# Attention units of a post-norm decoder: score rows as (sequence, query), values on both halves of the partitions, one output product, masks per token

## What is computed

```python
def _L2_xattn_ref(q, k, v, Wqkv, bqkv, Wo, bo, key_padding_mask, attn_mask, n_heads):
    proj = (jnp.concatenate([q, k, v], axis=1) @ Wqkv + bqkv)   # per head: qp, kp, vp
...
    scores = jnp.einsum('bqhd,bkhd->bhqk', qp, kp) / np.sqrt(dh).astype(qp.dtype)
    scores = jnp.where(mask, NEG, scores)
    attn = jax.nn.softmax(scores, axis=-1)
    y = jnp.einsum('bhqk,bkhd->bqhd', attn, vp)
    return y.reshape(Bq, T1, Dm) @ Wo + bo

x = _layernorm(x + _L0_attn_ref(x, ...))           # first mixing, "a0"
x = _layernorm(x + _L0_xattn_ref(ctx, x, ctx, ...))   # x0
x = _layernorm(x + _L0_ffn_ref(x, ...))            # two local-attention layers
x = _layernorm(x + _L1_attn_ref(x, W_qkv))         # a1
x = _layernorm(x + _L1_xattn_ref(x, ctx, ctx, ...))   # x1
x = _layernorm(x + _L1_ffn_ref(x, ...))            # "g", "gelu"
x = _layernorm(x + _L2_attn_ref(x, ...))           # "ema"
x = _layernorm(x + _L2_xattn_ref(x, ctx, ctx, ..., 32))  # x2
x = _layernorm(x + _L2_ffn_ref(x, ...))            # experts, top 1
x = _layernorm(x + _L3_attn_ref(x, ..., rel_emb))  # a3: scores + relative positions, causal
x = _layernorm(x + _L3_xattn_ref(x, ctx, ctx, mask, ...))  # x3
x = _layernorm(x + _L3_ffn_ref(x, ...))            # experts, top 2
```

## Time and profile before

| | |
|---|---|
| median of 3 runs | 818.88 us (815.96 to 819.70) |
| span of the profiled execution | 819.0 us |
| PE busy | 678.8 us, 83% |
| PEld busy | 523.5 us, 64% |
| DVE busy | 587.6 us, 72% |
| ACT busy | 462.2 us, 56% |
| POOL busy | 440.3 us, 54% |

### The profile page before, as it was taken

One profiled execution on the slowest core, in us unless ns is written; L12 is line 12 of the kernel. 1 busy time (PEld: TensorE's weight loads), 2 busy tenths in 40 slices (PEclk: granted clock), 3 DMA queues, 4 the chain that ended last, 5 costly groups with the idle time before them and its releaser, 6 DMA issues.

```text
span 819.0 us, 21672 instructions
## 1 busy us (share of the span) xinstructions
PE 678.8 (83%) x8144; PEld 523.5 (64%) x8144; DVE 587.6 (72%) x1594; ACT 462.2 (56%) x1136; POOL 440.3 (54%) x591
## 2 busy tenths in 40 slices
PE   5887968899988997999986799885978988955990
PEld 2576735777867785777743677645955666644990
DVE  4876969899888855788748987752557878862554
ACT  2235647487887662776722775443826756731671
POOL 3268726676655732254415877424666657553450
PEclk8667988799999998899995999867989989965995
DMA  8069000000000000000007700004124563004112
GB/s 340 11 222 136 2 1 2 1 1 2 2 1 2 1 2 1 2 3 3 4 1 87 224 3 2 3 13 98 46 59 155 182 184 103 3 30 98 58 38 84
DMA packets 49317, 45.21 MB, mean 55 GB/s; under 512 B 12896, under 2 KB 39648, under 8 KB 48704
## 3 DMA queue, kind: packets, MB, share of 16 engines
q1 hardware_dynamic: 46976, 39.23, 17.8%
q0 software_dynamic: 2240, 4.60, 1.6%
HBM read 30.94 MB, written 12.88 MB: 54 GB/s over the span
## 4 chain that ended last, share of the span: by engine, by line
PE 52%; DVE 18%; issue 10%; POOL 8%; ACT 5%; DMA 4%; SPq 1%; DVEq 0%; ACTq 0%; POOLq 0%
PE bank L889 6%; PE bank L868 6%; PE bank L877 5%; PE bank L904 3%; PE bank L1152 3%; PE bank L1078 3%; PE bank L1159 2%; PE bank L986 2%; DVE pairs L1721 2%; DVE pairs L1717 2%; POOL slots_x L2078 2%; PE bank L963 2%; DMA rel_scratch<-G 1%; PE bank L795 1%; PE bank L1012 1%
## 5 line engine op out<-in xcount | busy, mean ns | idle before, releaser
L2063 POOL TENSOR_TENSOR sm<-sm,mx 128x512 f32<-128x512 f32 x80 | 84.0, 1053 | 44.2 <-DVE mx L1638 43.7
L1251 ACT COPY pT<-bank 128x512 f32<-128x512 f32 x112 | 65.5, 585 | 46.3 <-PE bank L877 45.5
L1246 ACT ACTIVATE pr<-sm 128x512 f32<-128x512 f32 x112 | 70.2, 634 | 20.2 <-POOL sm L2063 19.6
L877 PE MATMUL bank<-W,pr 128*128 128x128 f32 x448 | 73.9, 290 | 8.3 <-ACT pT L1251 6.6
L2030 POOL TENSOR_SCALAR veps<-mv 128x1 f32<-128x1 f32 x104 | 25.3, 243 | 97.2 <-DVE mv L1573 97.1
L868 PE MATMUL bank<-pairs,Q 64*128 64x256 f32 x448 | 68.6, 427 | 2.2 <-DVE sm L1635 0.8
L2058 POOL TENSOR_TENSOR pairs<-KS,quad 128x512 f32<-128x512 f32 x48 | 50.5, 1054 | 35.5 <-ACT KS L1228 35.5
L2031 POOL TENSOR_TENSOR rstd<-veps,W 128x1 f32<-128x1 f32 x104 | 60.7, 584 | 8.7
L877 PEld LDWEIGHTS bank<-W,pr 128*128 128x128 f32 x448 | 52.0, 146 | 20.6 <-issue 10.8
L889 PEld LDWEIGHTS bank<-VX,pT 64*64 64x64 f32 x3072 | 52.1, 140 | 13.0 <-issue 6.8
L889 PE MATMUL bank<-VX,pT 64*64 64x9 f32 (+1 forms) x3072 | 56.5, 204 | 3.6 <-ACT pT L1251 1.6
(11 more groups left out here) (403 smaller groups left out, 1901.6 us busy)
## 6 DMA issues: line engine op xcount, KB each, us to landing
big<-gup SPq DMA_DIRECT2D x4, 1024.0 KB, 10.0
rel_scratch<-G SPq DMA_DIRECT2D x16, 256.0 KB, 2.7
W<-small SPq DMA_DIRECT2D x1, 3206.5 KB, 12.2
big<-early SPq DMA_DIRECT2D x2, 1557.0 KB, 8.4
slots_x<-zero SPq DMA_DIRECT2D x2, 1472.0 KB, 26.3
big<-down SPq DMA_DIRECT2D x8, 256.0 KB, 8.8
QM<-rel_scratch SPq DMA_DIRECT2D x16, 128.0 KB, 2.7
PM<-rel_scratch SPq DMA_DIRECT2D x16, 128.0 KB, 2.8
```

Source lines behind the costliest of these rows:

```text
L877: last = pe.transpose(tile(ps, p), pr[:, u % 2, 4 * h + p, :, :].rearrange("p b k -> p (b k)"), ident)
L1246: act.activation(pr[:, u % 2, 4 * h:4 * h + 4, :, :].rearrange("p g b k -> p b g k"), sm[:, 2 * (u % 2) + h, :].rearrange("p (b g k) -> p ...
L1251: act.copy(pT[:, u % 2, 4 * h:4 * h + 4, :], bank[BK[f"tu{h}"]][:, :].rearrange("p (h n) -> p h n", h=4)).then_inc(pt_ready, 1)
L2063: tt(v, v, bc(mx[:, slot, :], [P, 8, S], 2), ALU.subtract).then_inc(pcentered, 1)
```

## The change

The score rows become (sequence, query): one unit now computes its scores with eight products of 64x64 in place of four of 64x128, sequence b on its half of the partitions, and the two parities c of the heads as column halves. The exponent's output then needs no swap. The values of the two parities e stand on the two halves of the partitions (four products of 64 tokens in place of one; their bias is laid out the same way in a new table `BV`, filled by twelve small copies on DVE, and left out where it is zero). The 32 products of va give rows (sequence, query), in banks 6 and 7, and one reciprocal and one product of DVE normalise both banks. The output product is one product of 128x128 with the weights as they are, their rows only permuted at loading (sixteen loads, all at the start, with no memset before them). Masks are kept for each token row: half the columns, the two sequences loaded to the two halves of the partitions. The PSUM banks become one tensor; several steps change banks. The early routing of x3 becomes five planned steps (lg, e1, e2, rk, sl), and all ranks of the planner are new.

```diff
@@ plan @@
-            "pe.va": 0.95, "dve.on": 0.8, "pe.fo": 0.2, "act.o": 0.3, "pe.y": 0.5, "dve.re": 0.95, "pool.rs": 0.9,
+            "pe.va": 0.95, "dve.on": 0.5, "pe.fo": 0.2, "act.o": 0.3, "pe.y": 0.25, "dve.re": 0.95, "pool.rs": 0.9,
...
-CHAIN_BANK = {"k": 4, "v": 2, "q": 4, "tu0": 3, "tu1": 3, "va0": 6, "va1": 2, "fo": 5, "y": 7, "x": 5, "in": 2, "up0":
-              7, "up1": 3, "dn": 4}
-CHAIN_RANK = {"pe.sc": -4.0, "pe.v": 2.5, "pe.tu": -2.5, "pe.rel": -3.5, "dve.mix": 3.5, "act.ex": 4.0, "pe.va": 3.0,
-              "pe.y": 2.0, "pe.x": 3.5, "dve.re": 3.5, "pool.xb": 2.5, "dve.on": 2.0, "act.k": -4.0, "act.o": 3.5,
...
-STAGE_RANK, CHAIN_PATIENCE = 7, 0.02
+CHAIN_BANK = {"k": 4, "v": 7, "q": 4, "tu0": 3, "tu1": 3, "va0": 6, "va1": 7, "fo": 5, "y": 2, "x": 5, "in": 7, "up0":
+              5, "up1": 2, "dn": 4, "lg": 0, "rk": 6}
+CHAIN_RANK = {"pe.sc": 2.5, "pe.v": 9.5, "pe.tu": -5.0, "pe.rel": -11.0, "dve.mix": 6.0, "act.ex": 11.5, "pe.va": 3.0,
+              "pe.y": -2.5, "pe.x": -0.5, "dve.re": 5.5, "pool.xb": 19.5, "dve.on": 0.5, "act.k": -9.0, "act.o": -8.0,
...
+STAGE_RANK, CHAIN_PATIENCE = 9, 0.02
@@ SP, at the start @@
+            for b in range(2):
+                r = slice(b * S, (b + 1) * S)
+                for dst, rows_ in ((cap[:, 0, 0:MT], mrow), (m_pad, pad_rows), (m_ik, ik_rows)):
+                    sp.dma_start(dst[r], rows_.rearrange("p (t b) k -> p t b k", b=2)[r, :, b, :]).then_inc(masks_in, 16)
...
@@ SP, ahead of a3's trips @@
-            for name in ATT[4:]:
-                output_weights(name)
@@ PE @@
+            def values(ps, x, weights, wide):
+                v = weights.rearrange("p (r e n) -> p r e n", r=2 if wide else 4, e=2)
+                for b in range(2):
+                    for e in range(2):
+                        m = slice(b * S, (b + 1) * S)
+                        last = mm(ps[e * S:(e + 1) * S, m].rearrange("p (r n) -> p r n", r=2 if wide else 4), x[:, m], v[:, :, e, :],
+                                  start=True, stop=True)
+                return last
...
-                        for b in range(2):
-                            for r in range(2):
-                                rows = slice(r * S, (r + 1) * S)
-                                last = mm(ps[r][:, b * 256:(b + 1) * 256].rearrange("p (g k) -> p g k", g=4),
-                                          Q[rows, q2 + b, :, :].rearrange("p c q -> p (c q)"),
-                                          keys(u)[rows, :, b * S:(b + 1) * S], start=True, stop=True)
+                        for c in range(2):
+                            for b in range(2):
+                                for r in range(2):
+                                    rows, m = slice(r * S, (r + 1) * S), slice(b * S, (b + 1) * S)
+                                    last = mm(ps[r][m, c * 256:(c + 1) * 256].rearrange("p (g k) -> p g k", g=4),
+                                              own_q[rows, c, m], keys(u)[rows, :, m], start=True, stop=True)
...
-                        for b in range(2):
-                            for c in range(2):
-                                last = mm(ps[b * S:(b + 1) * S, 0:P], oT[:, t % 2, c * S:(c + 1) * S],
-                                          WO[:, a["i"] % 4, b, c, :], start=(c == 0), stop=(c == 1))
+                        mm(fill(BK["y"], y_used)[:, 0:P], oT[:, t % 2, :], WO[:, a["i"], :], start=True, stop=True).then_inc(y_full, 1)
@@ DVE @@
+            between = {0: token_shift, 1: turned_weights, 2: query_bias, 4: value_bias, 6: fading, 7: mask_x0}
...
-                        for b in range(2):
-                            dve.wait_ge(valued, due(valued))
-                            last = dve.reciprocal(rs[:, u % 2, b, :], o[b][:, :, d])
-                        link(last)
...
+                        dve.wait_ge(valued, due(valued))
+                        link(dve.reciprocal(rs[:, u % 2, :, :], o[:, :, :, d]))
+                        dst = OB[:, t % 4, :].rearrange("p (s e h d) -> p s e h d", e=2, h=8, d=d)[:, s_]
+                        tt(dst, o[:, :, :, 0:d], bc(rs[:, u % 2, :, :], [P, 2, 8, d], 3), ALU.mult).then_inc(on_ready, 1)
...
```

More of the change, by code:

```diff
@@ L249, in chain_jobs @@
                     jobs[(step, k, t, 0 if tail else s_, h)] = after
+        if name == "x3":
+            half = MT // 2
+            jobs["pe.lg", k, half, 0, 0] = [("act.x", k, t, 0, 0) for t in range(half)]
+            for step, t, needs in (("act.lg", half, ("pe.lg", half)), ("dve.e1", half, ("act.lg", half)),
+                                   ("dve.e2", MT - 2, ("dve.e1", half)), ("pe.rk", MT - 2, ("dve.e2", MT - 2)),
+                                   ("dve.sl", MT - 1, ("pe.rk", MT - 2))):
+                jobs[step, k, t, 0, 0] = [(needs[0], k, needs[1], 0, 0)]
         x_from = k
@@ L318, in chain_plan @@
             free[engine] = end[key]
-        if what in ("sc", "tu") and engine == "pe":
+        if what == "rk":
+            freed = ("dve.sl", key[1], MT - 1, 0, 0)
+        elif what in ("sc", "tu") and engine == "pe":
             freed = (CHAIN_FREES[what], key[1], key[2], key[3], 1 if what == "sc" else key[4])
@@ L847, in chain @@
                     if step == "v":
-                        mm(fill(BK["v"], v_split)[:, 0:P], tile(src, t), w(f"{name}.v"), start=True, stop=True).then_inc(v_full, 1)
+                        values(fill(BK["v"], v_split), tile(src, t), w(f"{name}.v"), wide).then_inc(v_full, 1)
                         at_["v", t] = due.now(v_split)
@@ L883, in chain @@
                         pe.wait_ge(v_split, at_["v", t])
[L884 removed]
+                        ps = fill_two([BK["va0"], BK["va1"]], on_ready)
                         for p in range(8):
[L886 to L892 removed]
+                            slot = p // 4 * 4 + p % 2 * 2 + p // 2 % 2
+                            for b in range(2):
+                                for e in range(2):
+                                    r, m = slice(e * S, (e + 1) * S), slice(b * S, (b + 1) * S)
+                                    last = mm(ps[e][m, slot * blk:(slot + 1) * blk], pT[r, u % 2, p, m],
+                                              V[r, (8 if wide else 16) * b + 8 * s_ + slot, :], start=True, stop=True)
+                        last.then_inc(valued, 1)
                         at_["on", t] = due.now(on_ready)
@@ L915, in chain @@
                         at_["x", t] = due.now(said)
-                        if name == "x3" and t == EARLY3 - 1:
-                            early_at = due.now(said)
-                        if name == "x3" and t == MT - 2:
-                            early_ranks()
-                    if step == "y" and name == "x3" and t == EARLY3 + 1:
-                        early_logits(early_at)
+                    if step == "lg":
+                        early_logits(max(at_["x", i] for i in range(EARLY3)))
+                    if step == "rk":
+                        early_ranks()
             def early_logits(x_at):
                 pe.wait_ge(xt_ready, x_at)
-                ps = fill(0, lg_ready)
+                ps = fill(BK["lg"], lg_ready)
                 for t in range(EARLY3):
@@ L932, in early_ranks @@
                 due(slot_ready)
[L933 removed]
+                ps = fill(BK["rk"], slot_ready)
                 incl = two[:, :, :].rearrange("p a b -> p (a b)").rearrange("p (e m) -> p e m", e=NE3)
@@ L1112, in context3 @@
                     for t in range(NT):
-                        last = mm(tile(ps, t), tile(CT, NT * hh + t), w("x3.v"), start=True, stop=True)
+                        last = values(tile(ps, t), tile(CT, NT * hh + t), w("x3.v"), True)
                     last.then_inc(v_full, 1)
@@ L1457, in turned_weights, with value_bias @@
                 last.then_inc(mixed_ready, 1)
-                tt(quad16[:, :], w("pair16", 0, 4), w("pair16", 4, 8), ALU.add)
-                tt(quad32[:, :], w("pair32", 0, 8), w("pair32", 8, 16), ALU.add).then_inc(quad_ready, 1)
-                dve.wait_ge(quad_ready, 1)
-            def rel_rows():
-                return tt(relp[:, :, :], bc(w("rel"), [P, 8, S], 1), bc(w("pair16"), [P, 8, S], 2), ALU.mult)
+                four = lambda v: v.rearrange("p (e i) -> p i e", e=2)
+                tt(quad16[:, :].rearrange("p (i e) -> p i e", e=2), four(w("pair16", 0, 4)), four(w("pair16", 4, 8)), ALU.add)
+                eight = lambda v: v.rearrange("p (s e i) -> p s i e", s=2, e=2)
+                tt(quad32[:, :].rearrange("p (s i e) -> p s i e", s=2, e=2), eight(w("pair32", 0, 8)), eight(w("pair32", 8, 16)),
+                   ALU.add).then_inc(quad_ready, 1)
+                dve.wait_ge(quad_ready, 1)
+            def value_bias():
+                dve.wait_ge(rest_in, 16)
+                for i, name in enumerate(BIASED_V):
+                    wide = att[name]["heads"] == 16
+                    rows_ = w(f"{name}.bv").rearrange("p (r e n) -> p r e n", r=2 if wide else 4, e=2)
+                    for e in range(2):
```

(11 more changed lines are left out.)

163 lines of the change are left out of this document (78 added, 85 removed).

## The result

Over the runs of the first comparison the changed kernel takes 812.87 us in the median (809.70 to 821.34) where the kernel before takes 821.72; the ratio is 0.9906 with a 95% interval of 0.9876 to 0.9935, so 7.7 us (5.3 to 10.2) were gained and 15.3 were forecast. The time lies in the forecast's wide range (791 to 817), just outside the narrow one (797 to 811), and the gain is half its size; the kernel before took 2.8 us more here than the 818.88 that the forecast starts from. The profiled execution has a span of 810.1 us at a mean granted clock of 0.867, against 819.0 at 0.875.

A forecast was written before the change was run, and what follows sets the result against it. PE was taken to set half the span (52% of the chain) and all of a1 and x1, no single engine the whole; terms summed to -15.3 us, 819.0 to 803.7, forecast 804 (797 to 811; wide range 791 to 817).

The forecast's parts named there:

- The output product: On PE, four products become one: 0.40 us saved (0.26 to 0.47), 48 times, including 0.10 of the step ahead.
- The value product: On PE, one product becomes four: 0.45 us from 0.33, plus 0.10 for the shape change; +0.22 on 40 tiles.
- The score product: On PE, four products become eight of 64x64: 1.02 us against 1.06, -0.04 for each of 56 units.
- The normalising step: On DVE, 0.79 us a unit becomes 0.48: 0.31 saved for each of 56 units, 17.4 us of DVE time.
- The value bias: Twelve small DVE copies, 2.1 us, in the first mixing's fifth round, where DVE waits 1.35 us: +0.5 (0 to +0.8).
- Masks and transfers: Mask tables of x0, x2, x3 halve: x2's gives -1.3 us, the others nothing; small mask transfers covered by 27 us slack.
- The order: All planner ranks new: the re-ordering not priced from the trace, value 0 with 4 us to both sides.
- The scatter's wait: First scatter on POOL, 0.73 us after POOL's last step, held by DVE's slots: +0.5 us (-0.7 to +1.5).
- (a): Rival: savings reach the end in full and the new order closes gaps as well; about 794 us, chance 0.12.
- (b): Rival: the waits only move, only the mask and the three ends stay; about 816 us, chance 0.15.
- (c): Rival: POOL's residual preparation comes later, residual add waits on DVE, 1.0 us for 24 tiles; 828 us, chance 0.08.
- (d): Rival: the score product's 16 weight loads run one after another, 56 x 1.1 = 63 us; 850 us, chance 0.03.

The follow-up runs named there:

- y_four: The changed kernel with the output product cut into four products again, two of them into unused columns; ratio 1.0053 to the kernel before, 12 us above the changed kernel.
- new_order: The kernel before, old layout, with the changed kernel's ranks, step costs, bank map and early experts' steps as jobs; ratio 0.9954 to the kernel before, 3.8 us faster.
- new_order_y1: The kernel before, old layout, under the changed kernel's order and with one output product in place of four; ratio 0.9797 to the kernel before, 16.8 us faster.
- no_recip: The changed kernel without the reciprocals of the normalisation, multiplying by constants instead; ratio 0.9832 to the kernel before, 6.1 us below the changed kernel, intervals overlapping.
- v_one: The changed kernel with the value product as one 128x128 product, as before; ratio 0.9851 to the kernel before, 4.5 us below the changed kernel, intervals overlapping.
- before_v4: The kernel before with the value product cut into four, the changed kernel's form; ratio 1.0036 to the kernel before, 3.0 us slower, if at all.
- on_pairs: The changed kernel with normalising as two reciprocals and two products again; ratio 0.9923 to the kernel before, 1.4 us above the changed kernel, not told from nothing.
- bias_late: The changed kernel with the value bias copies as six instead of twelve, moved behind the mask of x0; ratio 0.9873 to the kernel before.
- before_y1: The kernel before, in its own order, with one output product of 128x128 weights in place of four; ratio 0.9923 to the kernel before, 6.3 us faster.
- v_full: The changed kernel with its four value products each using all 128 columns of weights; ratio 1.0057 to the kernel before, 12 us above the changed kernel.

## Why the prediction was half right

**The step that failed.** The forecast added up what PE's steps gain and lose, let the sum through to the end almost whole, and gave the new order next to nothing. By its own terms the output product was worth 18.7 us (48 x 0.40 with a3's eight at half, and 0.37 at three ends), all else in the new layout cost 3.0 (v 7.9, value bias 0.5; scores -2.1, normalising -2.0, masks -1.3), and the order cost 0.5: in sum the 15.3, but for rounding. The runs show other sizes, under the new order: the output product is worth 12.1 us (y_four against the changed kernel) to 12.9 (new_order against new_order_y1), all else in the layout costs 8.1 us (y_four against new_order) to 9.0 (the changed kernel against new_order_y1), and the order alone gives 3.8. Each of these differences has an interval of 3 to 5 us to both sides. They add up to the 7.7 us that were gained: some 6 us short on the output product, 5 to 6 on the rest, and 4 better on the order.

**What bounds the kernel: right for a1 and x1.** Giving PE 0.3 us a tile back (y_four) gave all of the stretch's gain back; taking DVE time away (no_recip) moved nothing there.

**The output product: the slot nearly right, what reached the end too large.** 0.40 us was taken, between 0.26 and 0.47. Over the dense stretch its own slot has a mean of 0.60 before (0.59 in y_four) and 0.30 after: 0.22 us in about half of the places, 0.32 or more in the others. The 0.10 that the step ahead was to gain came in part. Between y_four and the changed kernel, which have the same order, that step gains 0.09 to 0.10 us in eight of thirteen places and nothing in the four where the weighted sum of values stands there. That makes 0.35 saved on average, close to what was taken. But the pace of the tiles gained 0.27, and the end 12.1 us, 0.25 for each of the 48: the rest turned into waits.

**The value product: the slot right, its price wrong.** 0.45 was forecast and 0.45 is the mean. The slot before was read as 0.33 from one place; its mean is 0.26, so the growth is 0.19 and not 0.12. The change of shape costs 0.09 where 0.10 was taken. The rule of the Trainium skill that was weighed there (page "TensorEngine Tiling (Array Packing)", section "Key Properties"), that a change of tiling mode drains the engine, agrees with the 0.32 of L885 against 0.23 in v_one. But in a1 and x1 the whole of it costs 0.03 us a tile and not 0.22, since it fills a wait for ACT, and 3.0 to 4.5 us at the end (before_v4, v_one), with intervals that reach down to zero. So the forecast for this stretch (0.22 us a tile gained, 0.27 measured) was right by luck, by two errors that cancel: y gave 0.27 and not 0.40, v took 0.03 and not 0.22.

**The score product: right**, 1.02 us as forecast, from one row of another stage with the same form.

**The normalising step: mis-sized, 17.4 us of DVE time against 5.0.** The step that failed is the price of 0.79 us a unit, which added the mean durations of instructions that overlap. The earlier trace rows show it themselves: 112 reciprocals of 177 ns make 19.8 us, but their busy time is 15.1. By busy time the reciprocals went from 15.1 to 13.7. As only 2 us of it were let through to the end, and on_pairs puts it at 1.4, it cost the forecast little.

**The value bias: too small, +0.5 taken within 0 to +0.8, +1.4 measured.** The twelve copies took 2.22 us (2.1 forecast). The step that failed is their cover: the 1.35 us that DVE waits for PE in the earlier trace rows is the wait of one execution. In others the same place shows 1.02 us, 0.83 or none, while the round with the copies takes 5.9 us always. So they cost 0.8 to 2.3 us of the round, mostly 1.3. The first output product comes at 49.2 to 50.8 us in nine executions with the copies in the round (49.9 in the mean), at 46.8 to 49.5 in six of the old layout (48.5) and at 47.2 in bias_late: 1.4 us later, and the other 1.3 of the 2.7 in the profiled pair are the lot of that pair.

**Masks and transfers: right.** The three steps of the x2 mask are 0.61, 0.44 and 0.43 us on the chain of waits, where the first two were 1.14 and 0.70; with a third like the second that is 1.1 us less (1.3 forecast).

```profile
425.92 0.61 DVE cap L1534
426.55 0.44 DVE cap L1535
427.02 0.43 DVE cap L1536
```

The mask of x0 stayed hidden. The first residual add still waits for PE (L861), and not for the small transfers.

**The order: the step that was wrong in kind.** It was given 0 with 4 us to both sides, as if it were a term of its own. Alone it gives 3.8 us. But it also seems to set what the other terms are worth: the shorter output product gives 6.3 us under the old order and 12.9 under the new one. The difference of 6.6 us has about 6 to both sides (an estimate from the intervals of the three runs); in the dense stretch the product gives 0.17 us a tile under the old order, 0.24 and 0.27 under the new one. And the new layout under the old ranks is slower than the kernel before. What is called the order here takes in the map of the banks and the planner's step costs; in the old layout no run separates them from the ranks. The scatter's wait of 0.73 us is down to 0.23 and no longer ends with DVE's slots, which is in the forecast's range:

```profile
717.94 1.12 POOL L2117 DMA_INDIRECT slots_x<-XB_id,slot  x1 [0.23 <-issue]
```

**Where the rest went.** Of the 8 to 9 us that the layout costs beside the output product, the runs of single terms show v at 3.0 to 4.5, the value bias at 1.4 to 2.7 and normalising at -1.4, and the rows of the mask show -1.1: together 1.9 to 4.7. The 3 to 7 us between lie within the intervals of the terms and aren't explained; the score product, the masks and the loads have no run of their own. By stage, the table puts 5.7 of the 6.5 us that the profiled pair misses ahead of the local layers, in the first mixing and x0. That is not to be trusted as it stands: bias_late, with the same chains, has x0 in 61.0 us, but x2 in 107.1 and a3 with x3 in 125.6 (65.3, 104.4 and 121.8 in the changed kernel). Which of x0, x2, a3 and x3 fell short stays open; a1 and x1 did not.

**The rivals.** (a), all gaps closed, did not come. (b), waits that only move, 816 us, is nearer to the time than the forecast, and its mechanism is what before_y1 shows under the old order; under the new one 12 to 13 us of the output product's saving arrived. (c) did not come: the residual add waits for PE (L1711). (d) did not come: 896 loads of 64x64 fill 31.5 us, 35 ns each, and no row shows them as late; its 56 x 1.1 is 62 and not 63.

## What to carry over

A shorter step on the busiest engine is worth only what the order of the work lets through to the next steps; price the two together, or put the longer step back under the new order to see what it is worth. A wait seen in one execution is no cover for added work: ask what ends it, and whether it is there when the engine that ends it runs a little faster; the wait at a loop's very end, ahead of a fixed hand-over, is the safer place. And when an engine's time is added up from a table, take busy time over count, not the mean duration, wherever neighbours overlap.

## What was not expected of the hardware

Four products with 64 columns of weights, on the two column halves of the array, take 0.38 to 0.51 us, the same four with 128 columns of weights 0.84 (v_full), with plain f32 weights of 128 rows. That the halves work at once would explain it; it is not shown apart from a shorter load. And the granted clock of a stretch moves between executions with the same instructions in the same order: over the chain of x0 it is 0.79 and 0.89 in two executions of the changed kernel, which take 65.3 and 63.9 us, and 0.89 in bias_late, which takes 61.0. Spreads of 1.4 to 4.4 us are as large as most of the terms that were to be measured there.
